# A graph network on one core: a bf16 edge sort, matmuls of ones ahead of the first product, residual sums on VectorE, and degree sums behind the turns

## What is computed

```python
edge_index = jnp.stack([src, dst])
h = jnp.maximum(_layernorm(x, axis=-1), 0.0)
x = x + _L0_gnn_ref(h, edge_attr_128, ..., edge_index)   # silu(edge @ We1 + be1) @ We2 + be2, times h[dst], summed by src; two-layer node network; + its input
h = jnp.maximum(_layernorm(x, axis=-1), 0.0)
x = x + _L1_gnn_ref(h, src, dst, W_init, W_fwd, W_bwd, W_self)   # three layers: mean over in- and out-neighbours, times W_fwd / W_bwd, joined, times W_self
...   # L2: one normalised convolution; L3: three of them and a last product
```

## Time and profile before

| what | value |
|---|---|
| median of 3 executions | 1182.57 us (1181.78 to 1183.78) |
| the profiled execution's own time | 1181.72 us |
| its span, first to last instruction | 1180.0 us |
| mean granted TensorE clock | 0.997 |
| TensorE busy | 1148.7 us (97%) |
| VectorE, ScalarE, GpSimd busy | 854.8, 676.1, 431.0 us |

### The profile page before, as it was taken

The page is one execution under the profiler, slowest core; times in us unless marked ns, Lnnn a source line. Parts: engine busy times, 40 slices in busy tenths (PEclk is TensorE's granted clock), DMA queues, the critical chain, the costliest instruction groups (busy, mean ns, idle before and its releaser), DMA issues.

```text
span 1180.0 us, 20814 instructions
## 1 busy us (share of the span) xinstructions
PE 1148.7 (97%) x6238; PEld 960.3 (81%) x6238; DVE 854.8 (72%) x1479; ACT 676.1 (57%) x1351; POOL 431.0 (37%) x546
## 2 busy tenths in 40 slices
PE   6999999999999999999999999999899999999998
PEld 3678887778888888888888888888879889897786
DVE  8898578877777777777777777777888325165665
ACT  3576665667667676766667676766734223141353
POOL 2002566766565655655565555553000000002000
PEclk9999999999999999999999999999999999999999
DMA  8623622222222222222222322222101203022101
GB/s 262 269 82 146 222 83 71 69 67 85 70 87 71 87 76 80 84 72 87 69 87 69 89 69 86 73 82 59 45 1 37 72 1 107 0 73 72 45 1 45
DMA packets 26966, 95.87 MB, mean 81 GB/s; under 512 B 6533, under 2 KB 6783, under 8 KB 22578
## 3 DMA queue, kind: packets, MB, share of 16 engines
q0 software_dynamic: 18592, 54.42, 15.5%
q1 hardware_dynamic: 8208, 40.84, 9.8%
q10 hardware_dynamic: 130, 0.13, 0.0%
HBM read 86.52 MB, written 8.85 MB: 81 GB/s over the span
## 4 chain that ended last, share of the span: by engine, by line
PE 74%; DVE 12%; ACT 7%; issue 4%; DMA 1%; POOL 1%; DVEq 0%; ACTq 0%; POOLq 0%
PE ps L1021 11%; PE ps L1022 11%; PE ps L1023 11%; PE ps L1014 8%; PE ps L1016 8%; PE ps L1015 8%; PE ps L1128 3%; PE ps L1127 3%; PE ps L1029 3%; PE ps L1028 3%; PE ps L1067 2%; ACT s L723 2%; PE ps L1132 2%; DVE msg L1696 1%; ACT s_hi L727 1%
## 5 line engine op out<-in xcount | busy, mean ns | idle before, releaser
L1021 PE MATMUL ps<-we_hi,s_hi 128*128 128x512 f32 x664 | 268.8, 405 | 0.0
L1022 PE MATMUL ps<-we_lo,s_hi 128*128 128x512 f32 x664 | 259.9, 391 | 0.0
L1023 PE MATMUL ps<-we_hi,s_lo 128*128 128x512 f32 x664 | 259.9, 391 | 0.0
L585 POOL DMA_INDIRECT xg<-h_dram,node_picks x166 | 177.1, 1067 | 96.2 <-POOL node_picks L575 65.6
L733 ACT ACTIVATE m_hi<-msg 128x512 fp32r<-128x512 f32 x166 | 105.0, 632 | 186.4 <-DVE msg L1696 185.0
L579 POOL DMA_INDIRECT rbf<-in_edge,edge_picks x166 | 175.1, 1055 | 50.5 <-issue 38.7
L1689 DVE TENSOR_TENSOR s_lo<-s,s_hi 128x1024 fp32r<-128x1024 f32 x83 | 101.6, 1225 | 78.3 <-ACT s_hi L727 78.3
L1701 DVE TENSOR_TENSOR m_lo<-msg,m_hi 128x512 fp32r<-128x512 f32 x166 | 114.7, 691 | 60.0 <-ACT m_hi L733 60.0
L1023 PEld LDWEIGHTS ps<-we_hi,s_lo 128*128 128x128 f32 x664 | 124.7, 188 | 27.6
L1021 PEld LDWEIGHTS ps<-we_hi,s_hi 128*128 128x128 f32 x664 | 125.0, 188 | 22.8
L1022 PEld LDWEIGHTS ps<-we_lo,s_hi 128*128 128x128 f32 x664 | 125.3, 189 | 20.6
(11 more groups left out here) (297 smaller groups left out, 2474.8 us busy)
## 6 DMA issues: line engine op xcount, KB each, us to landing
fold_dram<-folded SPq DMA_DIRECT2D x6, 1024.0 KB, 4.9
wstage<-fold_dram SPq DMA_DIRECT2D x6, 1024.0 KB, 4.8
plain<-in_fold_a SPq DMA_DIRECT2D x3, 1024.0 KB, 9.4
plain<-in_fold_b SPq DMA_DIRECT2D x3, 1024.0 KB, 11.4
stage<-in_fold_a SPq DMA_DIRECT2D x3, 1024.0 KB, 17.1
stage<-in_fold_b SPq DMA_DIRECT2D x3, 1024.0 KB, 24.3
w_raw<-in_nodew SPq DMA_DIRECT2D x3, 1024.0 KB, 10.6
wstage<-in_selfw SPq DMA_DIRECT2D x3, 1024.0 KB, 5.1
```

Source lines behind the costliest of these rows:

```text
L585: pool.indirect_dma_start(xg[t.slot][:, j], None, h_dram, bass.IndirectOffsetOnAxis(ap=node_picks[t.slot][:, j:j + 1], axis=0)).then_inc(x ...
L1021: pe.matmul(outp, lh, rh, start=False, stop=False, skip_group_check=True)
L1022: pe.matmul(outp, lh, rl, start=False, stop=False, skip_group_check=True)
L1023: return pe.matmul(outp, ll, rh, start=False, stop=False, skip_group_check=True)
```

## The change

1. Start. TensorE multiplies `ones32` by itself 18 times (`WARM`) as soon as that table is there. Product 0 is loaded in eight DMAs of 256 KB instead of two of 1 MB, and computed step by step `k` over four banks; the rank matmuls come behind its first step, not ahead of it.
2. Sort. The edge number, the source and the destination of an edge are packed as bits of two bf16 words, so a column needs two matmuls, not three. VectorE makes both `ended` words of even groups; of odd groups it makes the first, and ScalarE the second, by six activations of 128 columns (every second one). Even groups need nothing of ScalarE. The words are built by some eleven short operations on VectorE, six of them while it waits for the ranks; `slot_tables` has to take the words apart. No group is placed behind product 0; product 1 has ten.
3. Residual. The ten sums go from GpSimd to VectorE, same steps, between the one-hots and `s_lo`.
4. Degrees. The `degrow` units are gone: both column sums stand behind `turn(0)` and `turn(1)`. The low part of the adjacency (3,130 columns, L1845) goes there too, from ahead of the `mlp2` sums. The last chunk's normalisation comes behind `turn(1)` on ScalarE and behind `turn(0)` on VectorE.

```diff
+WARM = 18
 WHOLE = 3
-AFTER = (((), (), (0,), (1, 2, 3)), ((4, 5), (6, 7), (8, 9), (10,)), ((11, 12), (13, 14), (15, 16), (17, 18)),
-         ((19, 20), (21, 22), (23, 24), (25, 26)), ((27,), (), (), ()), ((), (), (), ()))
+AFTER = (((), (), (), ()), ((0, 1), (2, 3, 4), (5, 6, 7), (8, 9)), ((10, 11), (12, 13), (14, 15), (16, 17)),
+         ((18, 19), (20, 21), (22, 23), (24, 25)), ((26, 27), (), (), ()), ((), (), (), ()))
 REGION = 256
-KEY_ONE, KEY_SHIFT, KEY_P = 127 << 10, 13, 7
...
-IN_DEGREES, LAST = ("degrees", 1, 2), ("product", C - 1, 1)
-H1 = woven(turn(0), turn(1), IN_DEGREES, lin(0), turn(2), lin(1), back(0), turn(3), lin(2), back(1), turn(4), lin(3), back(2),
+LAST = ("product", C - 1, 1)
+H1 = woven(turn(0), turn(1), ("degrees", 0, 2), ("degrees", 1, 2), lin(0), turn(2), lin(1), back(0), turn(3), lin(2), back(1), turn(4), lin(3), back(2),
            lin(4), back(3), back(4))
...
-            load_factors(0)
+            for k in range(K):
+                for part, w in enumerate((a["fold_a"], a["fold_b"])):
+                    sp.dma_start(plain[0][:, part, k], w[0][:, k * F:k * F + F]).then_inc(quarter_in[k], 16)
...
-            def add_to_residual(t):
-                c, part = (t.c - 4) % C, (t.c - 4) // C
-                pool.wait_ge(late_small_in, 48)
-                if part:
-                    pool.wait_ge(res_ready, c + 1)
-                pool.tensor_tensor(x_res[:, c], x_res[:, c], row_b[0:NC] if part else h32[:, c],
-                                   op=ALU.add).then_inc(res_ready, 1)
-
-            def step_and_residual(t):
-                edge_step(t)
-                if t.reg is None and 4 <= t.c < 4 + 2 * C:
-                    add_to_residual(t)
-
-            steps(pool, STEPS, step_and_residual, lead=4 + 2 * C)
...
-                act.wait_ge(keys_ready, 1)
+                if i % ACT_EVERY == 0:
+                    return
+                act.wait_ge(ends_typed, 4)
                 act.wait_ge(hots_lo_made, i + 1)
-                for j in range(DUOS):
-                    n = i * DUOS + j
-                    act.activation(keyed[i % HOT_RING][:, j], hot_lo[i % HOT_RING][:, j], ACT.Copy,
-                                   scale=keys[:, n:n + 1].bitcast(F32)).then_inc(marks_made, 1)
+                for j in range(GROUP):
+                    n = i * GROUP + j
+                    act.activation(ended[i % HOT_RING][:, 1, j // 2, :, j % 2], hot_lo[i % HOT_RING][:, j // 2, :, j % 2],
+                                   ACT.Copy, scale=second_half[:, n:n + 1].bitcast(F32)).then_inc(marks_made, 1)
...
-            for c in range(C):
+            for c in range(C - 1):
                 deviation(1, c)
                 normed(1, c)
 
             for what, c, at in H1:
                 u = UNIT["h1"] + at
+                if (what, c) == ("degrees", 0):
+                    deviation(1, C - 1)
+                    normed(1, C - 1)
                 if what == "lin":
                     act.wait_ge(filled, u + 1)
...
-                pe.wait_ge(marks_made, (i + 1) * DUOS)
+                pe.wait_ge(marks_made, (i + 1) // ACT_EVERY * GROUP)
                 pe.wait_ge(ends_made, i + 1)
                 r = i % HOT_RING
                 for j in range(min(GROUP, ET - i * GROUP)):
-                    at = j % 2 * REGION
                     slots = hot_hi[r][:, j // 2, :, j % 2]
-                    pe.matmul(ps[:, 5, at:at + TILES], keyed[r][:, j // 2, :, j % 2], slots,
-                              start=False, stop=False, skip_group_check=True)
                     for v in range(2):
                         mm = pe.matmul(ps[:, 0, v * REGION:v * REGION + TILES], ended[r][:, v, j // 2, :, j % 2], slots,
                                        start=False, stop=False, skip_group_check=True)
...
+            def first_fold():
+                for k in range(K):
+                    pe.wait_ge(quarter_in[k], 32)
+                    for u in range(K):
+                        mm = pe.matmul(ps[:, 1 + u], plain[0][:, 0, k, u * P:u * P + P], plain[0][:, 1, k],
+                                       start=k == 0, stop=k == K - 1)
+                        if k == K - 1:
+                            mm.then_inc(fold_mm, 1)
+                    if k == 0:
+                        ranks()
+
+            pe.wait_ge(consts_ready, 1)
+            for _ in range(WARM):
+                pe.matmul(ps[:, 7, 0:P], ones32[:], ones32[:], start=True, stop=True)
+
+            first_fold()
+            pe.wait_ge(perm_zeroed, 1)
+            for m in range(1, FOLDS):
                 for u in range(K):
...
+                        pe.wait_ge(adj_whole, 1)
+                        if ones_by is by_two:
+                            pe.wait_ge(adj_split, 1)
                         for i in range(2):
-                            column_sums(unit(u + i), 1, i, ones_by)
...
+            dve.tensor_scalar(dst_up[:], dst_i[:], float(DST_FROM), None, ALU.add).then_inc(halves_made, 1)
+            dve.tensor_scalar(edge_half[:], edge_no[:], HALF_WORD, None, ALU.logical_shift_left).then_inc(halves_made, 1)
+            dve.tensor_scalar(src_bits[:], src_i[:], P - 1, HALF_WORD,
+                              ALU.bitwise_and, ALU.logical_shift_left).then_inc(halves_made, 1)
+            dve.wait_ge(halves_made, 1)
+            dve.tensor_scalar(odd_bit[:], dst_up[:], 1, 31, ALU.bitwise_and, ALU.logical_shift_left).then_inc(halves_made, 1)
+            dve.tensor_scalar(half_bit[:], dst_up[:], 2, 30, ALU.bitwise_and, ALU.logical_shift_left).then_inc(halves_made, 1)
+            dve.tensor_scalar(dst_bits[:], dst_up[:], 2, 23, ALU.logical_shift_right,
+                              ALU.logical_shift_left).then_inc(halves_made, 1)
...
+            dve.tensor_tensor(first_half[:], odd_bit[:], edge_half[:, 0:ET], op=ALU.bitwise_or).then_inc(halves_made, 1)
+            dve.tensor_tensor(low_bits[:], src_bits[:], dst_bits[:], op=ALU.bitwise_or).then_inc(halves_made, 1)
+            dve.wait_ge(ends_typed, 2)
+            dve.wait_ge(halves_made, 7)
+            dve.tensor_copy(ends16[:, 0, 0:ET], first_half[:].bitcast(F32)).then_inc(ends_typed, 1)
+            dve.wait_ge(halves_made, 8)
+            dve.tensor_tensor(second_half[:, 0:ET], low_bits[:], half_bit[:], op=ALU.bitwise_or).then_inc(ends_typed, 1)
+            dve.wait_ge(ends_typed, 4)
+            dve.tensor_copy(ends16[:, 1, 0:ET], second_half[:, 0:ET].bitcast(F32)).then_inc(ends_typed, 1)
...
-                for v in range(2):
+                for v in range(1 if i % ACT_EVERY else 2):
...
+                for v in range(2):
+                    dve.tensor_copy(word[v][:], ps[:, 0, v * REGION:v * REGION + TILES]).then_inc(perm_out, 1)
+                dve.tensor_scalar(number[:], word[0][:].bitcast(I32), HALF_WORD, EDGE_BITS,
+                dve.tensor_scalar(odd_i[:], word[0][:].bitcast(I32), 31, None, ALU.logical_shift_right).then_inc(perm_out, 1)
+                dve.wait_ge(perm_out, 3)
+                dve.tensor_scalar(slot_edge[:], number[:], float(-EDGE_FROM), 0.0, ALU.add, ALU.max).then_inc(table_ready, 1)
+                dve.tensor_scalar(slot_q[:], word[1][:].bitcast(I32), 23, 255,
+                                  ALU.logical_shift_right, ALU.bitwise_and).then_inc(perm_out, 1)
+                dve.tensor_scalar(slot_h[:], word[1][:].bitcast(I32), 31, None, ALU.logical_shift_right).then_inc(perm_out, 1)
+                dve.tensor_scalar(slot_s[:], word[1][:].bitcast(I32), HALF_WORD, P - 1,
+                                  ALU.logical_shift_right, ALU.bitwise_and).then_inc(perm_out, 1)
+                dve.wait_ge(perm_out, 6)
+                dve.scalar_tensor_tensor(out=half_up[:], in0=slot_q[:], scalar=2.0, in1=slot_h[:],
+                dve.wait_ge(perm_out, 8)
+                dve.scalar_tensor_tensor(out=dst_of[:], in0=half_up[:], scalar=2.0, in1=odd_i[:],
+                dve.wait_ge(perm_out, 9)
+                dve.tensor_scalar(slot_dst[:], dst_of[:], float(-DST_FROM), 0.0, ALU.add, ALU.max).then_inc(table_ready, 1)
...
+            def add_to_residual(t):
+                c, part = (t.c - RESIDUAL_FROM) % C, (t.c - RESIDUAL_FROM) // C
+                if part:
+                    dve.wait_ge(late_small_in, 48)
+                    dve.wait_ge(res_ready, c + 1)
+                else:
+                    dve.wait_ge(ln_act, 1 + C)
+                dve.tensor_tensor(x_res[:, c], x_res[:, c], row_b[0:NC] if part else h32[:, c],
+                                  op=ALU.add).then_inc(res_ready, 1)
...
+                if t.reg is None and RESIDUAL_FROM <= t.c < RESIDUAL_FROM + 2 * C:
+                    add_to_residual(t)
...
-            dve.wait_ge(adj_whole, 1)
-            dve.tensor_tensor(adj_lo[0][:], acc3, adj_hi[0][:], op=ALU.subtract).then_inc(adj_split, 1)
...
-                if c:
+                if 0 < c < 4:
                     coefs(1, c - 1)
-            coefs(1, C - 1)
+                if c == 3:
```

(12 more changed lines are left out.)

118 lines of the change are left out of this document (51 added, 67 removed).

## The result

Before 1183.44 us (median of 6 runs), after **1177.22 us** (median of 6, 1174.98 to 1179.1): ratio 0.9945, 95% interval 0.9931 to 0.9958, so 5 to 8 us faster. The forecast was 1167.3, and its range ended at 1173.5. The profiled execution took 1177.42 us (span 1175.6), 4.4 us less span than before.

The account below looks back on a forecast made before the run. TensorE was busy 97%, but VectorE and ScalarE led the groups from about 50 us. Prologue -3.1, residual -10.3 and degrees -1.9 sum to -15.3 us: 1182.57 - 15.3 = 1167.3 us, range 1161.5 to 1173.5.

Parts of the forecast that it names:

- The ones and the start: Kernel start: 36 passes over ones end near 7.2 us, VectorE goes on near 11.3, first group starts 1.5 us later.
- rival 6: Start: the ones do not raise the clock or end late, start 1.7 us later still, total 1169.0; chance 0.02.
- The groups: Sort in the prologue: VectorE saves 6.6 and 4.5 us, `fold_lo` waits grow 5.9, slot tables start at about 102.6.
- the prologue's term: Start, groups and slot tables together: -3.1 us, bounds -7.3 and +2.8.
- rival 1: Groups get shorter: marks cost 0.205 us or the start is not late; prologue gives 6.2 us, total 1164.2; chance 0.17.
- GpSimd's gathers follow directly ... and TensorE, with less to do, is ready before: Behind the slot tables: gathers set the time and TensorE is ready before, so the prologue's -3.1 us is kept.
- the forecast of 118.4: End of the prologue: `turn_rows` of step 1, called transpose 1 afterwards, comes near 118.4 us.
- rival 4: Prologue gaps from 66 us on: TensorE's clock falls, two units lose 2.7 us each, total 1172.7; chance 0.07.
- Residual sums: Edge stage: moving ten sums from GpSimd to VectorE, mostly into idle time, gives -10.3 us.
- Rival 3: Edge stage: VectorE's sums find no cover (+6.1) or hold up GpSimd's gathers (+6.9), total 1173.4 to 1174.2; chance 0.08.
- Steps of 8.34 us from step 4 on: Edge stage: every step from 4 on takes 8.34 us once GpSimd's residual sums are gone.
- Degrees: Behind the edge stage: the 2.23 us TensorE gap goes as both turns come first; -1.9 us, bounds 0 and -2.2.

Follow-up runs that it names:

- 18: 17 without the passes over ones (WARM = 0), everything else the same; 1164.91 us, ratio 0.9833.
- 17: Changed kernel with accumulators and edge weights 672 bytes higher, edge loop's buffers 4096, and GpSimd's gathers of steps 0 and 1 started early; 1164.7 us, ratio 0.9837.
- 1: Changed kernel with an unused 672-byte tile put back where one was dropped, below the edge loop's buffers; 1169.32 us, ratio 0.9888.
- 4: Changed kernel with the second bank of the last product ahead of the transpose of step 0 on TensorE; 1176.47 us, ratio 0.9940.
- 5: Kernel before with one part of the change alone, the ten residual sums on VectorE instead of GpSimd; 1173.91 us, ratio 0.9905.
- 2: Kernel before with one tile moved from below to above the edge loop's buffers, so these stand 672 bytes lower; 1188.67 us, ratio 1.0048.
- 6: Kernel before with one part of the change alone, the degree sums behind the first two turns; 1182.1 us, ratio 0.9981.
- 10: Changed kernel with the 672 unused bytes of 1 and the rank matmuls behind the second bank of the first quarter; 1170.21 us, ratio 0.9877.

## Why the prediction was wrong

*The ones and the start* (ends near 7.2, first group 1.5 us later): sizes a little off. 7.9 and +2.4 in this profile; in the others the 36 passes took 5.8 to 7.2 us. That ranks would come later than before was right. The ones are worth nothing (18 against 17). Of rival 6's further 1.7 us, 0.9 came.

*The groups*: the mechanism and nearly the size. The waits at `fold_lo` were to grow by 5.9 us and grew by 5.9; marks are 0.296 us apart, forecast 0.29. The slot tables were expected at 102.6 and start at 103.62; the 0.9 us of the start account for nearly all of it. The upper bound of the prologue's term was added up wrongly: with 3.2 for the start and 1.6 for the words it is +4.4, not +2.8. And of rival 1's two conditions only the cheap marks give its 3 us; a start that is not late gives 1.5.

*"GpSimd's gathers follow directly ... and TensorE, with less to do, is ready before"*: **this step failed.** I let the whole gain of the slot tables pass to transpose 1 and gave TensorE's earliness no price. But TensorE finishes product 4 earlier too, and so its 1 MB store is issued at 110.66 instead of 113.92 us; it went ahead of the second gather's rows, and transpose 0 followed that gather's issue by 3.94 us instead of 2.10. TensorE stood 2.36 us, and its clock fell where it was the leader. Both show at transpose 1: 1.8 us of the first, and 1.6 of the second (6.01 between the transposes against 4.4 in the profile of 1, and 4.43 in that of 4). Without them transpose 1 would have come at 117.7 (an estimate from these rows), where it is in the fast profiles; so the forecast of 118.4 was within reach. The two can't be added up to the end, though: with the stop and this fall gone (4), transpose 2 came only 0.57 us earlier. That the order of store and gather decides is read from all sixteen profiles; no run changed it alone.

The fall is rival 4's mechanism in another place: I priced it in the gaps from 66 us on, where the clock stayed at 1.00 in this profile, and not behind the groups. In seven of the later profiles it did fall in those gaps, at 99.9 to 101.3 us, where TensorE did not lead, and cost nothing that shows at transpose 1. The Trainium skill, "TensorE: Matmul & The Clock Gate", section "HAM oscillation", has the clock fall behind idle gaps; the rows agree.

The Trainium skill, "SBUF — State Buffer", section "SBUF: two separate sides", makes GpSimd wait while VectorE holds the shared port. 2.19 against 0.95 us agrees, in the prologue and not at the residual sums, where I weighed it (there the gather's issue under way took 0.95 as alone). But the kernel before had its 2.18 too. Its part here is that, counted from the slot tables, the second gather's issue ends 1.0 us later than in the profile of 1, and so behind the store's.

*Residual sums*: right. -9.42 us here, -10.1 where the buffers keep their place (5), forecast -10.3. Rival 3 did not come.

*"Steps of 8.34 us from step 4 on"*: **this is the larger failure**, +5.41 us over 65 steps. I costed the instructions of every edit and not the tile that it dropped. 672 bytes lower, the edge loop's buffers give TensorE's passes 0.083 us more a step, without a wait anywhere and at the full clock. Shown both ways by 1 and 2.

*Degrees*: right, -1.78 against -1.9, and about -2 alone (6). In part by luck: counted from the adjacency's transposes `lin(0)` came 2.6 us earlier (forecast 2.3), and 0.8 were lost behind it (forecast 0.4), with the 0.64 at `lin(2)` that I did not have.

*Behind the degrees* +1.6 us came back that I had at 0, 0.91 of it the wait in layer 2. The transfer behind it took 6.3 us instead of 5.3. It did so in twelve of the fifteen later kernels that hold the whole change, 5.8 us in one, and not in 17 and 18, nor in either part alone. What the transfer meets there stays open.

Open too: why places matter. Seen were 8.433 us (0, 64 and 2048 bytes), 8.420 (32), 8.407 (weights against the loop's buffers), 8.351 or 8.367 (672) and 8.307 (weights and accumulators against the loop's buffers). No run isolates the pair of buffers that matters, and each place was profiled once; 0.016 us of difference is also seen without a change of place (1 against 10). And that early gathers prevent the late transpose without the fall near 101 us is not shown, since the clock fell there in all three profiles that have them; that their rows were through 3 us before the store was issued speaks for it.

## What to carry to other kernels

When an edit adds or drops a tile, keep the addresses of the hot loop's buffers, or time both places: here that was worth as much as half of the largest edit. Price an engine that comes early like one that comes late: ask which transfers its results set off, whose data these get ahead of, and whether TensorE then stands long enough to lose its clock where it leads. Judge a loop's edit by the distance of one instruction over sixty rounds: with the changed kernel's buffers it was 8.433 us in all five profiles, while the totals of one kernel wander by 4 us. Differences of 0.02 us it does not settle.

## What was not expected of the hardware

- With no wait and a granted clock of 1.00, the same TensorE instructions took 8.307 to 8.433 us a step; all but 0.016 of that goes with buffer addresses.
- The 36 passes over ones took 5.8 to 7.2 us in the fifteen profiles that have them, all from 1.06 us on: the time at which the granted clock first rose differed by up to 3 us (4.3 to 7.3).
- A gather's issue on GpSimd took 0.95 us alone and 2.19 or 2.49 beside VectorE's subtractions; 0.1 us in the order of two starts goes with which.
- Two tenths of a microsecond went with which of a 1 MB store and a 64 KB gather moved first. With the store issued 0.3 us ahead of the end of the gather's issue, or later, the rows were through 1.2 to 1.3 us after that end; with the store issued 0.5 us ahead, 3.3 us after.
- A fall of TensorE's clock need not cost: in seven profiles it fell near 101 us, was hidden, and transpose 1 came at 117.3 to 118.2; in the seven without it and with the same order on TensorE, at 120.6 to 121.3.
